# Local feed-forward widening as three products of split operands, x parked in the output during the layers, bias and head scales by layer

## The reference

```python
def ffn_layer(x, g, bln, W1, b1, W2, b2):
    mu = x.mean(-1, keepdims=True)
    var = ((x - mu) ** 2).mean(-1, keepdims=True)
    xn = (x - mu) / jnp.sqrt(var + 1e-05) * g + bln
    hg = xn @ W1 + b1
    a, gate = jnp.split(hg, 2, -1)
    return a * jax.nn.gelu(gate, approximate=False) @ W2 + b2
...
for i in range(DEPTH):
    x = attn_layer(shift_tokens(x), Wqkv[i], q_scale[i], k_scale[i], Wo[i]) + x
    x = ffn_layer(shift_tokens(x), ln_g[i], ln_b[i], W1[i], b1[i], W2[i], b2[i]) + x
```

## Time and profile before

| | us |
|---|---|
| runs (3) | 2156.33, 2156.76, 2159.8; median 2156.76 |
| profiled execution | 2156.11 |
| its span, first to last instruction | 2154.2 |
| mean granted clock of TensorE | 0.992 |
| busy: TensorE, its weight loads | 2071.4, 1702.4 |
| busy: VectorE, ScalarE, GpSimd | 1704.6, 1358.3, 507.4 |
| DMA moved | 69.96 MB, mean 32 GB/s |

### The profile page before, as it was taken

One profiled execution on the slowest core, in us unless ns is written; L12 is line 12 of the kernel. 1 busy time (PEld: TensorE's weight loads), 2 busy tenths in 40 slices (PEclk: granted clock), 3 DMA queues, 4 the chain that ended last, 5 costly groups with the idle time before them and its releaser, 6 DMA issues.

```text
span 2154.2 us, 50541 instructions
## 1 busy us (share of the span) xinstructions
PE 2071.4 (96%) x16872; PEld 1702.4 (79%) x16872; DVE 1704.6 (79%) x4850; ACT 1358.3 (63%) x3950; POOL 507.4 (24%) x294
## 2 busy tenths in 40 slices
PE   5999999999998998999999999999999999999988
PEld 4777877887886676888888888888888888888877
DVE  6786786787675598898888888988889888988882
ACT  3776576567564355676667666766676666766652
POOL 2111111111111432232223222322223222322220
PEclk9999999999999999999999999999999999999999
DMA  3000000000000400021102001201120111011000
GB/s 120 9 9 1 7 11 1 7 12 1 6 26 1 157 11 13 16 70 33 53 14 72 22 25 52 71 14 34 52 72 14 34 53 59 17 33 53 14 14 20
DMA packets 47053, 69.96 MB, mean 32 GB/s; under 512 B 9157, under 2 KB 33781, under 8 KB 46581
## 3 DMA queue, kind: packets, MB, share of 16 engines
q1 hardware_dynamic: 44469, 62.21, 9.6%
q10 hardware_dynamic: 2368, 4.98, 0.6%
HBM read 50.54 MB, written 1.05 MB: 24 GB/s over the span
## 4 chain that ended last, share of the span: by engine, by line
PE 54%; DVE 4%; DMA 3%; issue 3%; ACT 2%; POOL 1%; SPq 0%; DVEq 0%; ACTq 0%; POOLq 0%
PE ps_loc L1665 17%; PE ps_loc L1771 9%; PE ps_loc L1742 6%; PE ps_loc L1781 4%; PE ps_loc L1715 4%; PE ps_loc L1704 4%; PE ps_loc L1731 4%; PE ps_loc L1684 3%; DMA late<-y_all 2%; POOL rnorm L2572 1%; PE ps_loc L1325 1%; DMA w_raw<-in_ffn_Wqkv_dram 1%; DVE w_low L2186 1%; DVE norm L2194 1%; ACT prob_loc L1994 1%
## 5 line engine op out<-in xcount | busy, mean ns | idle before, releaser
L2572 POOL TENSOR_TENSOR rnorm<-norm_floor,half_loc 128x32 f32<-128x32 f32 x48 | 299.5, 6239 | 585.2 <-DVE norm_floor L2197 461.9
L1665 PE MATMUL ps_loc<-w_high,xT 128*128 128x512 f32 x1152 | 379.2, 410 | 0.7 <-ACT qk L1973 0.6
L1994 ACT ACTIVATE prob_loc<-prob_loc,top_loc 128x128 f32<-128x128 f32 x768 | 298.4, 398 | 44.9 <-DVE top_loc L2261 42.6
L1771 PE MATMUL ps_loc<-xnT_loc,w 128*128 128x256 f32 (+1 forms) x1056 | 252.6, 385 | 3.1 <-DVE kT_loc L2329 1.8
L702 ACT ACTIVATE prob<-prob,new_top 128x256 f32<-128x256 f32 x512 | 252.2, 497 | 0.0
L1665 PEld LDWEIGHTS ps_loc<-w_high,xT 128*128 128x128 f32 x1152 | 203.5, 188 | 50.5 <-issue 9.3
L2261 DVE CUSTOM_DVE_ANT_0 prob_loc<-ps_loc,const,rnorm 128x128 f32<-128x128 f32 x768 | 219.0, 347 | 26.2 <-PE ps_loc L1704 24.4
L1986 ACT ACTIVATE qT_loc<-ps_loc 128x512 f32<-128x512 f32 x96 | 57.3, 597 | 286.9 <-PE ps_loc L1684 286.9
L1665 PE MATMUL ps_loc<-w_low,xT 128*128 128x512 f32 x576 | 227.4, 395 | 0.0
L1771 PEld LDWEIGHTS ps_loc<-xnT_loc,w 128*128 128x128 f32 (+1 forms) x1056 | 190.7, 189 | 29.8 <-DVE kT_loc L2329 3.0
L907 DVE CUSTOM_DVE_ANT_0 prob<-ps_cross,bias 128x256 f32<-128x256 f32 x512 | 184.6, 420 | 20.4 <-PE ps_cross L478 10.8
(11 more groups left out here) (205 smaller groups left out, 4394.8 us busy)
## 6 DMA issues: line engine op xcount, KB each, us to landing
w_raw<-in_ffn_Wqkv_dram SPq DMA_DIRECT2D x24, 512.0 KB, 5.7
w_raw<-in_ffn_Wqkv_dram SPq DMA_DIRECT2D x24, 256.0 KB, 4.1
wo<-in_ffn_Wo_dram SPq DMA_DIRECT2D x24, 256.0 KB, 3.8
v_mid<-v_even SPq DMA_DIRECT2D x24, 256.0 KB, 3.4
v_mid<-v_odd SPq DMA_DIRECT2D x24, 256.0 KB, 3.7
w<-in_ffn_W_dram SPq DMA_DIRECT2D x12, 341.0 KB, 4.6
w<-in_ffn_W_dram SPq DMA_DIRECT2D x6, 640.0 KB, 4.9
ctx_raw<-in_ctx_dram SPq DMA_DIRECT2D x12, 256.0 KB, 2.7
```

Of the source, the lines that this page charges most:

```text
L1665: ins = pe.matmul(ps[:, DENSE + j % 2, :], xT[:, px, kk, t * P:(t + 1) * P], wqkv[pw][:, kk, col:col + 512], start=kk == 0 and n == 0, sto ...
L1771: ins = pe.matmul(ps[0:n, DENSE + m % 2, part * T:(part + 1) * T], w1[:, kk, col:col + n], xnT[:, kk, :], start=kk == 0, stop=kk == KD - 1)
L1994: ins = act.activation(pr, pr, ACT.Exp, bias=top[:, h, t:t + 1], scale=-1.0, accum_out=total[:, h, t:t + 1])
L2572: pool.tensor_tensor(rnorm[:, b % 2, t, :], norm2_floor[:, :], half[:, :], ALU.pow).then_inc(rnorm_done, 8)
```

## The change

Widen becomes three fp32r products: high part of xn by high part of W1, high by low, low by high, for each of the two halves of the contraction. For it
- ScalarE's xn_out writes the rounded copy xnT_high and the fp32 xnT, four operations instead of two (count xnT_copied), and VectorE's new xn_low subtracts one from the other into the place of xnT (count xnT_done), right behind the share of pair 5.
- ScalarE's new widening_high, at the end of slot 0, waits for w1_in and makes four rounded copies of 128x682; GpSimd's new widening_low subtracts them from w1 in its place, between rotate of batch 1 and norm of batch 0. Widen 0 of batch 0 waits for that instead of w1_in.
- To make room x_all is written to the output's memory when the layers begin (park_x), and read back into the place of the q/k/v weights after the last projection (fetch_x), for the sum at the end. Bias and head scales are loaded layer by layer (load_bias behind w1, load_head_scale behind w2).
- Widen 5 makes 128 instead of 106 columns (with zeros between).

```diff
@@ SyncE
             def ffn_weights(L, i):
                 sp.wait_ge(f_full, L)
                 k.load_layer_weights(sp, i, "w1")
+                sp.wait_ge(b2_done, L)
+                k.load_bias(sp, i)
                 sp.wait_ge(f2_full, L)
                 k.load_layer_weights(sp, i, "w2")
 
+            def park_x():
+                sp.wait_ge(y_out, 2 * LAYER)
+                sp.dma_start(out_dram, k.x[:, :, :]).then_inc(k.x_moved, 16)
+
+            def fetch_x():
+                sp.wait_ge(k.x_moved, X_PARKED)
+                sp.wait_ge(qkv_full, (LAYERS + 1) * LAYER)
+                sp.dma_start(k.x_back[:, :, :], out_dram).then_inc(k.x_moved, 16)
...
             def layer(L, i, first, last):
+                if first:
+                    park_x()
                 middle(L, 1)
                 shift(L, 0)
                 if not first:
                     ffn_weights(L, i)
+                if not last:
+                    sp.wait_ge(tables_done, L + LAYER)
+                    k.load_head_scale(sp, i + 1)
                 middle(L, 2)
@@ TensorE, widen
                     if b == 0:
-                        pe.wait_ge(w1_in, a + LAYER)
-                    pe.wait_ge(xnT_done, a + U)
+                        pe.wait_ge(w1_split_low, a + LAYER)
+                    pe.wait_ge(xnT_copied, a + U)
...
-                    for kk in range(KD):
-                        ins = pe.matmul(ps[0:n, DENSE + m % 2, part * T:(part + 1) * T], w1[:, kk, col:col + n], xnT[:, kk, :],
-                                        start=kk == 0, stop=kk == KD - 1)
+                    for n, (px, pw) in enumerate(WIDE_PARTS):
+                        if m == 0 and px == LOW:
+                            pe.wait_ge(xnT_done, a + U)
+                        for kk in range(KD):
+                            ins = pe.matmul(ps[:, DENSE + m % 2, part * T:(part + 1) * T], w1_parts[pw][kk][:, col:col + P],
+                                            xnT_parts[px][:, kk, :], start=n + kk == 0,
+                                            stop=n + kk == len(WIDE_PARTS) + KD - 2)
@@ ScalarE
-                for kk in range(KD):
-                    ins = act.activation(xnT[:, kk, :], ps[:, DENSE, kk * T:(kk + 1) * T], ACT.Identity,
-                                         bias=vec[:, V_FB + kk:V_FB + kk + 1], scale=vec[:, V_FG + kk:V_FG + kk + 1])
-                ins.then_inc(xnT_done, U)
+                for dst in (xnT_parts[HIGH], xnT):
+                    for kk in range(KD):
+                        ins = act.activation(dst[:, kk, :], ps[:, DENSE, kk * T:(kk + 1) * T], ACT.Identity,
+                                             bias=vec[:, V_FB + kk:V_FB + kk + 1], scale=vec[:, V_FG + kk:V_FG + kk + 1])
+                ins.then_inc(xnT_copied, U)
+
+            def widening_high(L, first):
+                if first:
+                    act.wait_ge(k.x_moved, X_PARKED)
+                    for part, kk in itertools.product(range(2), range(KD)):
+                        act.activation(w1_parts[part][kk][:, FF:GATE_REST], zero.broadcast_to([P, GATE_REST - FF]), ACT.Copy)
+                act.wait_ge(w1_in, L + LAYER)
+                for h in range(W1_PIECES):
+                    kk, cols = w1_piece(h)
+                    act.activation(w1_parts[HIGH][kk][:, cols], w1[:, kk, cols], ACT.Copy).then_inc(w1_split_high, w1_step(h))
...
                     weights_high(L + LAYER, 11)
+                if b == 0:
+                    widening_high(L, not ffn)
@@ VectorE
+            def xn_low(a):
+                dve.wait_ge(xnT_copied, a + U)
+                dve.tensor_tensor(xnT_parts[LOW][:, :, :], xnT[:, :, :], xnT_parts[HIGH][:, :, :], ALU.subtract)\
+                    .then_inc(xnT_done, U)
...
                 share(a, 5)
+                if ffn:
+                    xn_low(f)
@@ GpSimd
+            def widening_low(L):
+                for h in range(W1_PIECES):
+                    kk, cols = w1_piece(h)
+                    pool.wait_ge(w1_split_high, L + (h + 1 if h < W1_PIECES - 1 else LAYER))
+                    pool.tensor_tensor(w1_parts[LOW][kk][:, cols], w1[:, kk, cols], w1_parts[HIGH][kk][:, cols], ALU.subtract)\
+                        .then_inc(w1_split_low, w1_step(h))
...
                 rotate(L + U, 1)
+                widening_low(L)
```

More of the change, by code:

```diff
@@ L143, in __init__ @@
         self.ctx = ctx
-        self.x = self.sb("x_all", [P, B * TT, D])
+        self.x_moved = self.sem("x_moved")
+        self.dve_held, self.held = self.sem("dve_held"), self.sem("held")
+        with ExitStack() as shared:
+            self.x = self.sb("x_all", [P, B * TT, D], ctx=shared)
+        first = self.sb("w1_high0", [P, W1_COLS], F32R)
+        self.xnT_high = self.sb("xnT_high", [P, KD, T], F32R)
+        self.sb("x_rest", [P, B * TT * D - W1_COLS - KD * T])
+        self.w1_high = [first]
         self.y = self.sb("y_all", [P, B * TT, D])
@@ L175, in place_layer_weights @@
     def place_layer_weights(self):
+        with ExitStack() as shared:
+            self.x_back = self.sb("x_back", [P, B * TT, D], ctx=shared)
         self.w_high = self.sb("w_high", [P, KD, 3 * INNER], F32R)
@@ L1533, in local_layers @@
         xn = sb("xn_loc", [P, TT, D])
-        xnT = sb("xnT_loc", [P, KD, T])
+        with ExitStack() as shared:
+            xnT = k.sb("xnT_loc", [P, KD, T], F32, shared)
+        xnT_parts = (k.xnT_high, sb("xnT_low", [P, KD, T], F32R))
+        w1_parts = (k.w1_high, [k.w1_low[:, kk, :] for kk in range(KD)])
         k.lin_place.close()
@@ L1577, in after, with w1_piece, w1_step @@
             return n + 1 if n < last else U
+        X_PARKED, X_BACK = 32, 48
+        W1_PIECES = 2 * KD
+        def w1_piece(h):
+            kk, part = divmod(h, 2)
+            return kk, slice(GATE_REST, W1_COLS) if part else slice(0, FF)
+        def w1_step(h):
+            return 1 if h < W1_PIECES - 1 else LAYER - W1_PIECES + 1
         def after_piece(h):
@@ L2541, in _ @@
             pool.memset(half[:, :], -0.5)
-            for buf in (zero[:, :], late[0:1, :, :], w1[:, :, FF:GATE_REST]):
+            for buf in (zero[:, :], late[0:1, :, :]):
                 ins = pool.memset(buf, 0.0)
@@ L2572, in rotate, with loads @@
                     pool.tensor_tensor(rnorm[:, b % 2, t, :], norm2_floor[:, :], half[:, :], ALU.pow).then_inc(rnorm_done, 8)
+            def loads(count):
+                return count if isinstance(count, int) else pool.snap(count)
+            def widening_low(L):
[4 more added lines that the diff above has]
+                        .then_inc(w1_split_low, w1_step(h))
             def norm(a, i, b):
@@ L2630, in _ @@
             last = slice((B - 1) * TT, B * TT)
[L2631 removed]
+            pool.wait_ge(k.x_moved, X_BACK)
+            pool.tensor_tensor(k.x_back[:, last, :], k.x_back[:, last, :], k.y[:, last, :], ALU.add).then_inc(x_mid, 1)
 STAGES = (cross_attention, local_layers)
```

71 lines of the change are left out of this document (41 added, 30 removed).

## The result

The changed kernel took 2222.64 us, the median of four runs (2219.52 to 2223.96), beside 2156.55 for the kernel before on the same chip: a ratio of 1.0303 (95% interval 1.0285 to 1.032), slower by 66 us. The prediction was 2217, with a range of 2186 to 2240, and slower with 0.95. The profiled execution took 2222.82 us, its span 2221.0, 66.8 more than before.

What follows compares the result with a forecast made beforehand. It took TensorE's own stream to set the pace in the local layers. To the profiled 2156.11 us it added 63 (wait) + 8.5 (clock) - 11 (slots) = +60.5, 2216.6; the median lies 0.65 higher: 2217, range 2186 to 2240.

Steps and rivals of the forecast that it cites:

- The new wait: Behind slot 0 of layers 2 to 6, TensorE's transposes wait for ScalarE's q copy: 12.7 us five times, 63 us.
- The clock: Behind each new wait TensorE's granted clock is near half: 1.7 us lost each, 8.5 in all, bounds 0 and 9.
- What a slot keeps: With a longer chain ahead of widening, a slot nets about 0.6 us; 19 slots gain 11 us.
- The raw gain: TensorE's 66 fp32r widening matmuls at 0.122 us save 1.4 to 1.8 us a slot, 34 to 43 over 24 widenings.
- estimate from the four passes: Three single passes replacing fp32's four in the widening would save 2.4 us a slot, 58 in all; not used in the sum.
- Edits at no cost: GpSimd's subtractions, parking and fetching x, bias and head-scale loads are hidden; without the wait, subtractions cost up to 3 us.
- tail: After the last slot, two more ScalarE operations (+1) against faster TensorE matmuls (-1.8): about -1 us, left in the rounding.
- B: Rival: the faster matmul rate counts in full, 1.4 to 1.8 us a slot over 24: 2190 us; chance 0.14.
- C: Rival: slots give nothing or lose, the longer ScalarE and VectorE chain costing 0.5 us in each: 2240 us; chance 0.13.
- D: Rival: an fp32r widening product costs as much as a half fp32 one, 0.215 us: 2330 us; chance 0.03.
- A: Rival: not slower, w1 transfers land before ScalarE needs its queue, no wait left: 2143, down to 2114 us; chance 0.05.

Runs made afterwards that it cites:

- e1: The kernel before plus only ScalarE's wait for the layer's w1 transfers at the end of slot 0, no copies or split: 2217.62 us, ratio 1.0286.
- e2: The changed kernel with w1 transfers of layers 2 to 6 issued ahead of slot 0's token shift: 2147.18 us, ratio 0.9959 to the kernel before.
- e8: e6 with GpSimd's four subtractions also waiting for VectorE's last product of q and k with rnorm for slot 1: 2136.22 us, ratio 0.9898.
- e6: e2 with one fp32 copy out of PSUM, rounding from SBUF, and the first block's high-row products ahead of its low-row ones: 2140.46 us, ratio 0.992.
- e5: e2 with GpSimd's four subtractions moved from slot 0 into slot 1, behind its norm of slot 0: 2156.48 us, ratio 0.9993.
- e4: e2 without the fp32 copy of xn and the subtraction, the third product taking the rounded xn instead of the low part: 2136.02 us, ratio 0.9903.
- e9: e2 with e6's copies alone (fp32 out of PSUM, rounding from SBUF), order of products unchanged: 2148.61 us, ratio 0.9954.

## Why the prediction was right, and which terms were off

**The new wait: right.** Forecast 63 us in five places, measured 63.9; 12.7 each, measured 12.8 on the mean and 13.1 at most. Its chain held link by link: issue behind the shifts, the small w1 transfer landing last (5.6 us in layer 3; 5.6 to 7.0 in rows 8), four copies of 0.69, then the q copy, and the fifth transpose group behind that. e1 shows the wait as the cause, e2 shows the issue's place in SyncE's queue as the cause of the wait.

**The clock: the size held, in part by luck.** Forecast 1.7 a wait, 8.5 in all, with 9 as its upper bound. From the restart of the transposes to the scores behind them the five slots of the kernel after took 3.27, 3.60, 3.34, 3.26 and 3.41 us, where the same half takes 1.84 in a slot without a wait (3.68 from start to scores in e2, halved): 1.4 to 1.8 a wait, 7.7 in all, and the scores are back at their full pace. In e1 the low clock lasted longer, 3.7 to 5.9 us behind the restart against 2.9 to 3.5 here, and transposes and scores together lost 2.5 a wait, 12.5 in all, over the upper bound. Why it rose later there the runs don't show. The stretch that I priced it by had nine matmuls, this one sixteen transposes; that the price fits is luck. The rule that every idle gap is paid again is wider than these traces: behind the wait of 0.35 us shown below, at 1223.49, the clock read 1.00.

**What a slot keeps: near the forecast, by the chain that it named.** Forecast 0.6 us a slot, 11 in 19 slots. By layer, slot 0 to 1 won 0.5 to 0.8, slot 3 to next 0 0.4 to 0.8 and slot 2 to 3 between 0.0 and 0.9; over all 17 intervals without a wait it is 8.7 us, 0.51 each. The five with the wait are 70.1 us longer than before's, 1.5 less than wait and clock together. So 10.2 in all. The raw gain was forecast as 1.4 to 1.8 a slot, from 0.122 a matmul. Slot 3's widening in layer 2, to be read against rows 3:

```profile
1222.41 0.50 PE L1826 MATMUL ps_loc<-xnT_high,w_high 128*128 128x256 f32 x2
1222.75 0.40 PE L1826 MATMUL ps_loc<-xnT_high,w_low 128*128 128x256 f32 x2
1223.49 0.50 PE L1826 MATMUL ps_loc<-xnT_low,w_high 128*128 128x256 f32 x2 [0.35 <-DVE xnT_low L2396]
...
1228.29 0.51 PE L1826 MATMUL ps_loc<-xnT_high,w_high 128*128 128x256 f32 x2
...
1235.05 2.32 PE L1795 MATMUL ps_loc<-wo,qT_loc 128*128 128x256 f32 x10
```

Inside a block two matmuls are 0.23 to 0.24 us apart, 0.12 each, as priced, but the first two of a block take 0.32 to 0.35 to the next start, 0.1 more; there are five block starts in a slot. Block by block, from the start of one to the start of the work behind it, the widening took 2.13, 1.59, 1.52, 1.60 and 2.24, 9.08 us with the wait of 0.35, against 9.83 before. So the raw gain was 1.1, under my lower bound of 1.4. What is kept is set further on, as argued: by how late the third block starts and how much is won behind that. Its links, with ScalarE's and VectorE's rows of that slot:

```profile
1220.43 1.01 ACT L2074 ACTIVATE xnT_high<-ps_loc,vec 128x256 fp32r<-128x256 f32 x2
1221.33 1.03 ACT L2074 ACTIVATE xnT_loc<-ps_loc,vec 128x256 f32<-128x256 f32 x2
```

```profile
1222.76 0.68 DVE L2396 TENSOR_TENSOR xnT_low<-xnT_loc,xnT_high 128x512 fp32r<-128x512 f32 x1
1227.75 0.48 DVE L2404 SCALAR_TENSOR_TENSOR kT_loc<-ps_loc,vec,gate 128x256 f32<-128x256 f32 x1 [1.34 <-ACT gate L2094]
```

From the first xnT copy to the third block it is now 7.86 us (1220.43 to 1228.29), before 7.28 (1205.34 to 1212.62): 0.58 late, where 0.5 was forecast, and behind the gated product of 1227.75, the one that was named. From there to the work behind the widening it is 6.76 (to 1235.05) against 7.78: 1.02 won, where 1.1 was forecast. Together 14.62 against 15.06: 0.44 won in this slot, where 0.6 was forecast. The prediction's estimate from the four passes for true FP32 of the Trainium skill ("FP8 and Floating Point Precision", TensorE Precision Notes) was 2.4 us a slot; the measured 1.1 is under half of it.

**Edits at no cost: not all of them.** GpSimd's subtractions were indeed hidden behind the wait in layers 2 to 6. Where there is no wait they cost something, but not as I had it: not by delaying rstd but by standing beside a product of VectorE. In e2 the group of that product is 8.3 us dearer than before (66.9 against 58.6), and e8, where it is at 58.6 again, is 4.2 us faster than e6. Layer 1 has no wait, so the kernel after pays there itself:

```profile
835.21 2.58 DVE L2303 TENSOR_TENSOR qk<-qk,rnorm 128x1024 f32<-128x1024 f32 x1 [1.58 <-POOL rnorm L2652]
```

```profile
835.09 6.89 POOL L2663 TENSOR_TENSOR w_low<-w,w_high 128x682 fp32r<-128x682 f32 x4
```

Parking, fetching back, bias and head scales left no wait of TensorE among the longest.

**What wasn't in the sum.** The first transposes of the local stage came at 837.84 instead of 833.86, the first shift at 838.42 instead of 834.44. 2.7 of these 4.0 us were there already at the linear attention's first load (703.99 against 701.28 before), ahead of which the change adds no work; e2 and e5, with the same code ahead, have 699.55 and 699.31, so this is a difference between executions. The other 1.3 is the change's: the product just shown, 1.23 before, for which TensorE's first transposes wait (4.0 us against 2.7). From that load to the first shift it is 134.3 to 134.4 us in the five kernels that have this collision in layer 1 (after, e2, e4, e6, e9) and 132.9 to 133.2 in the six that don't.

Added up by the starts of the transposes: 3.98 ahead of the first, 70.11 more in the five intervals with the wait, 8.69 less in the seventeen others, 1.40 behind the last: the 66.80 of the spans. Against the prediction's +60.5: the wait 0.9 dearer than forecast, the clock 0.8 cheaper, the slots 0.8 short of their 11, the start 4.0, the tail 1.4 where about -1 had been left in the rounding. So what the forecast missed is mostly start and tail; the tail wasn't traced to a row.

**The rivals.** B (the rate in full) and C (the slots lose) fall with these: 10.2 over all slots is neither 38 won nor 12 lost. D falls with 0.12 us a matmul. A (the transfers land in time) is what e2 made true: the prediction gave it 2143, and e2, where the copies end 1.9 us ahead of the transposes' start at 1284.02, took 2147, with VectorE's longer product in six layers.

## What to carry to other kernels

A wait that one engine takes over from another costs what is queued behind it on the new engine, and its price is set by the queue that issues the awaited transfer: compare the issue's place with the moment from which the waiting engine is needed, and move the issue before moving anything else. If a chain of splits stands ahead of matmuls, put the products that need only its first result in front, for every part of the block. And when a wait is removed, look again at what it was hiding, since work that ran in its shadow lands beside something else. Read gains between marks of the engine that sets the pace: here the issues of another engine moved by themselves.

## What the runs showed of the hardware

VectorE's products of two SBUF operands and GpSimd's subtractions held each other up: 1.22 us became 2.67 in e2, 2.60 in e6, 2.58 in layer 1 of the kernel after and 2.41 in e5 at another product, and was 1.23 where the subtractions stood elsewhere (e5's product with rnorm, and e8); the four subtractions took 6.89 to 7.40 us beside such a product and 5.93 in e8 without. The groups over the whole span, product with rnorm in e2 and in e8 (busy us, mean ns of one):

```profile
L2304 DVE TENSOR_TENSOR qk<-qk,rnorm 128x1024 f32<-128x1024 f32 x48 | 66.9, 1394 | 18.9 <-issue 17.3 <-POOL rnorm L2653 1.6
```

```profile
L2308 DVE TENSOR_TENSOR qk<-qk,rnorm 128x1024 f32<-128x1024 f32 x48 | 58.6, 1221 | 18.9 <-issue 17.3 <-POOL rnorm L2657 1.6
```

The added 1.45 us is one subtraction (5.93 / 4 = 1.48). The Trainium skill ("SBUF — State Buffer", SBUF: two separate sides) says that the two engines share one pair of ports, that a VectorE operation with two SBUF inputs and a GpSimd operation that reads SBUF take it as an exclusive lock, and that whichever comes second is blocked for the whole instruction. The trace agrees: the product began 0.04 us behind the first subtraction and was one subtraction late. VectorE's addition with one operand in PSUM at 1282.81, beside the same subtractions, took the 0.68 us that it takes elsewhere.
